# Attention values and softmax sums taken in 32-column quarters of TensorE, with a wide reciprocal on VectorE

## The reference

```
h = layernorm(x) * (1 + ca) + sa
x = x + ga * attention(h)          # 16 heads of 16; 4 sink keys and the last 128 keys
h = layernorm(x) * (1 + cb) + sb
x = x + gb * (shared_ffn(h) + sum over the top 2 of 16 experts of weight * expert(h))
```

## Time and profile before

| what | us |
|---|---|
| median of 3 runs | 353.09 (351.51 to 356.67) |
| the profiled execution | 351.6 |
| its span | 349.8 |
| PE busy | 280.7 (80%) |
| DVE busy | 232.1 (66%) |
| POOL busy | 204.4 (58%) |
| ACT busy | 162.4 (46%) |

### The profile page before, as it was taken

One profiled execution on the slowest core, in us unless ns is written; L12 is line 12 of the kernel. 1 busy time (PEld: TensorE's weight loads), 2 busy tenths in 40 slices (PEclk: granted clock), 3 DMA queues, 4 the chain that ended last, 5 costly groups with the idle time before them and its releaser, 6 DMA issues.

```text
span 349.8 us, 6292 instructions
## 1 busy us (share of the span) xinstructions
PE 280.7 (80%) x1665; PEld 218.9 (63%) x1666; DVE 232.1 (66%) x899; ACT 162.4 (46%) x518; POOL 204.4 (58%) x254
## 2 busy tenths in 40 slices
PE   4897889888989898988873998999899898986000
PEld 4174467655857486756642897889889787875000
DVE  0468477997789876997894654644354576862990
ACT  3042552278135743457213355555455565753540
POOL 3604107738775577648657364556556468783981
PEclk9998996999789987999988799999999999998755
DMA  7939101123615529802275663555557678757894
GB/s 265 325 95 361 33 2 60 62 77 121 195 46 165 166 92 340 191 15 85 85 211 186 204 173 107 151 153 162 150 154 222 192 243 262 233 171 274 287 358 163
DMA packets 41438, 59.80 MB, mean 171 GB/s; under 512 B 5092, under 2 KB 29880, under 8 KB 41404
## 3 DMA queue, kind: packets, MB, share of 16 engines
q1 hardware_dynamic: 34312, 39.91, 38.8%
q0 software_dynamic: 6528, 17.90, 14.3%
q10 hardware_dynamic: 564, 1.59, 1.3%
HBM read 33.57 MB, written 25.80 MB: 170 GB/s over the span
## 4 chain that ended last, share of the span: by engine, by line
PE 49%; DVE 23%; issue 8%; DMA 7%; ACT 5%; another core or an unknown queue 2%; SPq 2%; POOL 1%; DVEq 1%; POOLq 0%; ACTq 0%
PE bank L1225 15%; PE bank L1235 7%; PE bank L890 7%; PE bank L1050 5%; PE bank L1083 5%; PE bank L1027 2%; PE bank L1103 2%; DVE h_sb L1367 2%; DVE st L1341 2%; PE bank L933 2%; DMA ht<-in_L_attn_x_dram 2%; ACT pt_win L674 2%; DVE xs L1389 1%; ACT p_win L717 1%
## 5 line engine op out<-in xcount | busy, mean ns | idle before, releaser
L646 POOL DMA_INDIRECT ys<-pt_win,row_i x72 | 71.5, 992 | 52.2 <-issue 25.9
L1225 PE MATMUL bank<-ht,w_now 128*128 128x128 f32 x576 | 79.2, 282 | 5.6 <-issue 4.5
L593 POOL DMA_INDIRECT slots<-h_sb,slot_i x64 | 63.2, 988 | 31.3 <-DVE slot_i L1438 16.0
L1225 PEld LDWEIGHTS bank<-ht,w_now 128*128 128x128 f32 x576 | 73.0, 198 | 6.8 <-issue 5.1
L1736 DVE TENSOR_TENSOR act_t<-bank,sg 128x128 f32<-128x128 f32 x72 | 20.9, 291 | 49.0 <-ACT sg L841 33.6
L674 ACT ACTIVATE ht<-bank 128x256 f32<-128x256 f32 x104 | 39.9, 383 | 22.4 <-PE bank L890 12.9
L1235 PE MATMUL bank<-w_dn,act_t 128*128 x144 | 45.2, 396 | 4.3 <-DVE act_t L1736 3.8
L674 ACT ACTIVATE pt_win<-bank 128x256 f32<-128x256 f32 (+1 forms) x88 | 37.3, 423 | 21.0 <-PE bank L1235 8.3
L1083 PE MATMUL bank<-w_route,ht 128*128 128x272 f32 x128 | 41.5, 452 | 4.3 <-ACT ht L674 1.8
L890 PE MATMUL bank<-ident,p_win 128*128 128x128 f32 x198 | 36.0, 277 | 5.5 <-issue 2.8
L890 PEld LDWEIGHTS bank<-ident,p_win 128*128 128x128 f32 x198 | 26.6, 143 | 19.2 <-issue 7.7
(11 more groups left out here) (260 smaller groups left out, 490.1 us busy)
## 6 DMA issues: line engine op xcount, KB each, us to landing
p_win<-slots SPq DMA_DIRECT2D x67, 129.0 KB
slots<-pads SPq DMA_DIRECT2D x28, 129.0 KB
xs<-in_L_attn_x_dram SPq DMA_DIRECT2D x3, 1024.0 KB
wmod_sb<-ys SPq DMA_DIRECT2D x12, 256.0 KB
w_gu<-ys SPq DMA_DIRECT2D x10, 256.0 KB, 2.8
mod_bc<-mod_rows_out SPq DMA_DIRECT2D x4, 512.0 KB, 5.4
w_dn<-in_L_ffn_w_down_dram SPq DMA_DIRECT2D x1, 2048.0 KB
h_sb<-ys SPq DMA_DIRECT2D x8, 256.0 KB
```

The source lines that it names most:

```text
L593: pool.indirect_dma_start(out=slots, out_offset=bass.IndirectOffsetOnAxis(ap=slot_i[:, k, j:j + 1], axis=0), in_=h_sb[:, j, :], in_offset= ...
L646: pool.indirect_dma_start(out=ys, out_offset=bass.IndirectOffsetOnAxis(ap=row_i[:, col:col + 1], axis=0), in_=y_sb[:, k, :], in_offset=Non ...
L1225: last = mm(bank[2 + k % 2][:, half * P:(half + 1) * P], w_now[:, k % 2, c, half * M:(half + 1) * M], ht[:, k, c, :], start=(c == 0), stop ...
```

## The change

`at_values` is turned round. The values of two heads stand in 32 stationary columns, with zeros beside them (`v_pad`), and the transposed probabilities are the moving operand. Each product writes 32 of the 128 output partitions, so that four products fill the four quarters of a bank. The output comes out transposed, as `at_project` needs it: `at_out_t` and ACT's copy are gone. The sums come from a second set of products with ones in place of values (`at_sums`, `ones_pad`, `sink_ones`), 256 moving columns each. They give every sum 16 times over, in the layout of the output, and DVE takes the reciprocal of all 128x256 elements. The setup gets the matching constants, and the products of the few sink rows (`small_values`) get their sums from matmuls of their own.

The order moves too. On PE: `at_sums`, `at_values`, `gate_up(b, 5)`, `rank`, `at_project`, `tr`, `act_tr`, `down`. On DVE: `at_norm(b + 1)` goes in front of `activation(b, 4)`, `at_normalise` in front of `ranked` and `placed`, and the statistics of the next batch's first tiles behind `activation(b, 5)`. On POOL: `last_norm` goes ahead of `scale(b, 6)`, and `rsqrt(b, 2)` ahead of the next batch's `scale` calls. On ACT: `h_copy(b, 5)` and `act_copy(b, 5)` go ahead of `centre(b + 1, 0)` and `centre(b + 1, 1)`.

```diff
@@ constants and tiles
-    DA = DH + 1
+    PAIR_STEP = 2 * DH
+    V_HALF = CH * PAIR_STEP + DH
-        sink_v = sb("sink_v", [H * SINKS, B * H * DA])
+        sink_v = sb("sink_v", [H * SINKS, B * D])
+        sink_ones = sb("sink_ones", [H * SINKS, D])
-        v_aug = sb("v_aug", [P, H, DA])
+        v_pad = sb("v_pad", [P, 2 * V_HALF])
+        ones_pad = sb("ones_pad", [P, 3 * DH])
-        rden = sb("rden", [P, H])
+        rden = sb("rden", [P, D])
@@ pool
+                if b + 1 < B:
+                    last_norm(b + 1)
                 if b == 0:
                     rsqrt(b, 3)
                 scale(b, 6)
...
                 if b + 1 < B:
-                    last_norm(b + 1)
                     rsqrt(b + 1, 0)
+                rsqrt(b, 2)
+                if b + 1 < B:
...
                     scale(b + 1, 0)
                     scale(b + 1, 1)
-                rsqrt(b, 2)
@@ act
                 tanh(b, 5)
-                act.wait_ge(S["at_ot"], b + 1)
-                copy(o_t[:].rearrange("p c n -> p (c n)"), bank[6][:, 0:D]).then_inc(S["at_ots"], 1)
+                h_copy(b, 5)
+                act_copy(b, 5)
                 if b + 1 < B:
                     centre(b + 1, 0)
                     centre(b + 1, 1)
-                act_copy(b, 5)
-                h_copy(b, 5)
@@ pe
+            def at_sums(b):
+                wait_apart(pe, S["at_pts"], b * (HG + 1) + HG + 1)
+                for c in range(C):
+                    mm(bank[6][:, c * P:(c + 1) * P], sink_ones[:, c * P:(c + 1) * P], pt_sink[:], start=(c == 0),
+                       stop=False, skip_group_check=True)
+                for u in range(2):
+                    for i in range(4):
+                        last = mm(bank[6][32 * i:32 * i + 32, 0:D], ones_pad[:, (1 - u) * DH:(3 - u) * DH],
+                                  pt_win[:, 2 * i + u::CH, :], start=False, stop=(u == 1), skip_group_check=True)
+                last.then_inc(S["at_den"], 1)
+
+            def at_values(b):
+                for c in range(C):
+                    mm(bank[7][:, c * P:(c + 1) * P], sink_v[:, ds(b * D + c * P, P)], pt_sink[:], start=(c == 0),
+                       stop=False, skip_group_check=True)
+                for c in range(C):
+                    for u in range(2):
+                        for i in range(4):
+                            v_at = u * (V_HALF - DH) + (c * 4 + i) * PAIR_STEP
+                            last = mm(bank[7][32 * i:32 * i + 32, c * P:(c + 1) * P], v_pad[:, v_at:v_at + PAIR_STEP],
+                                      pt_win[:, c * CH + 2 * i + u, :], start=False, stop=(u == 1),
+                                      skip_group_check=True)
+                last.then_inc(S["at_o"], 1)
@@ order on pe
-                at_values(b, range(0, H // 2))
+                at_sums(b)
+                at_values(b)
+                gate_up(b, 5, b == 0)
                 rank(b * GPB, 0, GROUP, b * TPB + 2)
-                at_values(b, range(H // 2, H))
-                gate_up(b, 5, b == 0)
-                at_out_t(b)
-                act_tr(b, 5, b == 0)
                 at_project(b)
                 tr(b, 5)
+                act_tr(b, 5, b == 0)
@@ dve
             def at_normalise(b, at):
+                dve.wait_ge(S["at_den"], b + 1)
+                at.done(v.reciprocal(rden[:], bank[6][:, 0:D]))
                 dve.wait_ge(S["at_o"], b + 1)
-                ob = bank[7][:, 0:H * DA].rearrange("q (h s) -> q h s", h=H)
-                at.done(v.reciprocal(rden[:], ob[:, :, DH]))
-                v.tensor_tensor(o_n[:], ob[:, :, 0:DH], rden[:].unsqueeze(2).to_broadcast([P, H, DH]), ALU.mult)\
+                v.tensor_tensor(o_t[:].rearrange("p c n -> p (c n)"), bank[7][:, 0:D], rden[:], ALU.mult)\
                     .then_inc(S["at_on"], 1)
@@ order on dve
                 add_y(b, 3)
+                if b + 1 < B:
+                    at_norm(b + 1, at)
                 activation(b, 4)
...
+                at_normalise(b, at)
                 ranked(b * GPB)
                 placed(b * GPB)
-                if b + 1 < B:
-                    at_norm(b + 1, at)
-                    norm_stats(b + 1, 0, ln)
-                at_normalise(b, at)
                 if b == B - 1:
                     early_table(0)
                 activation(b, 5)
+                if b + 1 < B:
+                    norm_stats(b + 1, 0, ln)
```

More of the change, by code:

```diff
@@ L135, in norm_of @@
             return 0 if j < 2 else 2 if j == TPB - 1 else 3 if b == 0 and j == TPB - 2 else 1
-        norms = ["a0", "00", "10", "30"]
-        for b in range(B):
+        norms = ["a0", "00", "10", "a1", "30", "01", "20", "11"]
+        for b in range(1, B):
             norms += [f"a{b + 1}", f"0{b + 1}", f"2{b}", f"1{b + 1}"] if b + 1 < B else [f"2{b}"]
@@ L750, in own_values @@
                 act.wait_ge(S["at_v"], b + 1)
-                copy(v_aug[:, :, 0:DH], bank[6][:, 0:D].rearrange("p (h s) -> p h s", s=DH))\
+                copy(v_own, bank[6][:, 0:D].rearrange("p (m u s) -> p u m s", u=2, s=DH))\
                     .then_inc(S["at_vs"], 1)
@@ L989, in small_values @@
                 for b in range(B):
-                    last = mm(bank[3][0:NB, 0:H * DA], sm_pt[:, b, :], sink_v[:, b * H * DA:(b + 1) * H * DA],
-                              start=(b == 0), stop=(b == B - 1))
+                    mm(bank[3][0:NB, 0:D], sm_pt[:, b, :], sink_v[:, b * D:(b + 1) * D], start=(b == 0), stop=False,
+                       skip_group_check=True)
+                for b in range(B):
+                    last = mm(bank[3][0:NB, D:D + H], sm_pt[:, b, :], head_block[:], start=False, stop=(b == B - 1),
+                              skip_group_check=True)
                 last.then_inc(S["sm_ps"], 1)
@@ L1042, in at_probs_t @@
                 last.then_inc(S["at_pt"], 1)
[L1044 to L1051, removed]
-                if heads[-1] == H - 1:
-                    last.then_inc(S["at_o"], 1)
@@ L1055, in at_out_t @@
-            def at_out_t(b):
-                pe.wait_ge(S["at_on"], b + 1)
-                for k in range(C):
-                    last = transpose(bank[6][:, k * P:(k + 1) * P],
-                                     o_n[:].rearrange("q h s -> q (h s)")[:, k * P:(k + 1) * P])
-                last.then_inc(S["at_ot"], 1)
-            def at_project(b):
-                pe.wait_ge(S["at_ots"], b + 1)
+            def at_sums(b):
[8 more added lines that the diff above has]
+                last.then_inc(S["at_den"], 1)
@@ L1064, in at_project @@
+            def at_project(b):
+                pe.wait_ge(S["at_on"], b + 1)
                 for k in range(C):
@@ L1521, in small_normalise @@
                 dve.wait_ge(S["sm_ps"], 3)
-                so = bank[3][0:NB, 0:H * DA].rearrange("q (h s) -> q h s", h=H)
-                ch.done(v.reciprocal(sm_r[:], so[:, :, DH]))
-                v.tensor_tensor(sm_o[:], so[:, :, 0:DH], sm_r[:].unsqueeze(2).to_broadcast([NB, H, DH]), ALU.mult)\
+                so = bank[3][0:NB, 0:D].rearrange("q (h s) -> q h s", h=H)
+                ch.done(v.reciprocal(sm_r[:], bank[3][0:NB, D:D + H]))
+                v.tensor_tensor(sm_o[:], so, sm_r[:].unsqueeze(2).to_broadcast([NB, H, DH]), ALU.mult)\
                     .then_inc(S["sm_or"], 1)
@@ L1668, in _ @@
                 add_y(b, 3)
+                if first:
+                    dve.wait_ge(ld_x[1], 16)
+                if b + 1 < B:
+                    at_norm(b + 1, at)
                 activation(b, 4)
@@ L1795, in _ @@
                 gated(d)
-N_CONST = 32
+N_CONST = 34
 RT_CH = 9
```

17 lines of the change are left out of this document (11 added, 6 removed).

## The result

The changed kernel took 355.19 us (median of 20 runs, 352.48 to 358.69), the kernel before beside it 354.57 (20 runs, 350.37 to 358.97). The ratio is 1.0055, with a 95% interval from 1.0028 to 1.0081: half a per cent slower, far inside the 2% called no change. The predicted 357 was 1.8 us too high. But 357 was worked out as 3.7 us on top of a kernel before of 353.1; in this comparison the kernel before took 354.6, and the ratio makes the change worth some 2 us. The direction was right, but the case given the best chance, pairs, isn't what happened.

What follows compares the result with a forecast made beforehand. Bound: PE from the sinks' product through the projection, then DVE. Batches -0.1, -0.2, 0.0, +2.5, setup +0.1 and clock +1.4 give +3.7 on 351.6 profiled: 355.3, plus 1.5 for the median: 356.8, said as 357; range 348 to 366.

Steps and rivals of the forecast that it cites:

- pairs: Quarter products on PE run two at a time: sums 1.94 us, values 1.84, stage 5.4; chance 0.42.
- What bounds the kernel: Batch 1's chain runs on PE from 88.28 to 98.65, then on DVE; a faster PE alone gives at most 2.76 us.
- four at a time: Rival: all four quarters overlap on PE, stage 3.3 us, DVE bounds; 349 profiled, 350.7; chance 0.22.
- Changes of shape: Switching product shapes on PE costs 0.15 us each, five per stage: 0.75 us.
- Reciprocal: 256 columns on DVE take 1.76 us, 1.5 more per batch, needing only the sums; hidden if quarters overlap two at a time.
- The old fall of the clock: Half clock during the heads' narrow products goes if wide streams keep it up; a fall cost 3.0 us at the projection's end.
- A new fall in PE's idle: PE idles some 3 us before `down(b, 6)` in batches 0 to 2, clock falls: 0.7 for two of them, +1.4 us.
- `rank` behind `gate_up(b, 5)`: `rank` is seen 6.65 us after the stage's start; `ranked`, `placed` and DVE's queue wait, total 13.65 us.
- POOL: "nothing": Scatters wait for `placed`, some 4 us later, yet fit with two rsqrts and two scales before the next batch: no cost.
- Batch 3: No half clock to regain, and `early_table(0)` waits for the count from `rank`: `activation(3, 5)` starts 2.5 us later.

Runs made afterwards that it cites:

- The test in one quarter: Changed kernel with all quarter products written to the first 32 rows of their bank; 366.1 us, one run.
- the narrow one: Changed kernel with a reciprocal of 16 columns in place of 256; 344.82 us, ratio 1.0034 to the kernel before.
- filler alone: Changed kernel plus six bf16 products of 512 columns in PE's idle before `down` of tile 6, every batch; 341.60 us, ratio 0.9980 to the kernel before.
- rank first: Changed kernel with `rank` between `at_sums` and `at_values`, `ranked` and `placed` before `at_normalise`; 339.13 us, ratio 0.9786 to the kernel before; repeat 337.97, 0.9803.

## Why the prediction was right, and where it was wrong

- **What bounds the kernel**: right. The edited stage was on the path; with it faster, DVE's idle went.
- **Pairs** (chance 0.42): wrong. Sums and values take 1.0 us each and not 1.94 and 1.84. The step that failed is the ordering argument, that the second record of an f32 product must wait for the first before the next quarter can go. The test in one quarter (3.64 us) and the rows of the changed kernel (1.07) say four at a time. The figure that the prediction cited beside it (the Trainium skill, "TensorE: Matmul & The Clock Gate", Part 3) points the right way: it gives 2.38 times for three column tiles. The runs here give 3.4 for four (3.64 / 1.07); none has three.
- **Changes of shape**: right as a sum. The stage is 3.3 us, what the rival had for it with 0.15 each.
- **Reciprocal**: right in price (1.76 us) and place. It waits 0.46 us for the sums. Its load isn't what ate the gain, as the narrow one shows.
- **The old fall of the clock goes**: right in all batches.
- **A new fall in PE's idle**: right in kind; it shows in `gate_up` of tile 7 in batches 0, 1 and 3 (62.2, 100.2, 179.4 us), and one tile later in batch 2 (143.4). But its price of +1.4 us isn't there: filler alone moved no spacing, and all that `gate_up` gained by it was idle (1.82 us) until DVE's `h_sb`, late behind POOL.
- **`rank` behind `gate_up(b, 5)`**: this order costs, as forecast, but by another way: rank first gives 5.6 us back. On DVE there is no wait for `rank` in batch 1, since the reciprocal and the product stand in front; the cost comes through POOL.
- **POOL: "nothing"**: wrong, and the most instructive step. The prediction said that four scatters, two roots and two scales "fit before the next batch needs them", and looked at the scales' consumer alone. The first consumer is `h_tile(b, 7)`, which waits for the root. On POOL's queue, one by one from `slot_i` at 94.16: the issues end at 99.7, the roots at 100.96, and DVE wants them at 99.9. The trace of before had the means to see it: slots 4 us later by its own estimate, four scatters 1.27 us apart (92.49 to 97.30), and `centred` right behind `activation(b, 6)`.
- **Batch 3**: +0.8 us to the end of `activation(3, 6)` and 0.7 to the start of `activation(3, 5)` (7.04 us after the sinks for 6.30), where pairs had +2.5 and four at a time +0.7.
- **The number**: the rival of four at a time had 350.7 us: -1.3, -2.0, -1.3 in batches 0 to 2. The first stretch gave more, -2.4, -2.7, -1.8. What it lacked is POOL's +2.0 in each of three batches and up to 0.9 behind it, which has no cause here. Its sum with these is 350.7 - 2.3 + 6.0 + 2.1 = 356.5, or 355.1 without the clock's 1.4. That 357 is close is luck in large part: products too dear by 2.1 us a batch and a queue too cheap by 2 us cancel, and the kernel before came out 1.5 us slower than the 353.1 that the sum started from. Against that kernel the forecast was +3.7 us, and the measured ratio gives some +2.

## What to carry to other kernels

When a step is moved later, count what is queued behind it on every engine that it feeds, one instruction at a time, and ask which consumer of that queue comes first, not which seems the natural one. Three waits stood here one behind the other (POOL's root, the landing of a scatter behind bulk loads, DVE beside POOL's scales); taking the first two away, from behind, gave 3 us of spacings in the end (113.9 to 110.8), and putting the small row product and the slots ahead of the wide work gave 5.6 (to 108.3). And the releaser that a profile names is only the last that it sees: where a wait has two conditions, look up the landing time in the queue's rows too.

## What the hardware showed

- Products in four column quarters run side by side even in f32: 32 records of 128 columns in 1.08 us, 3.68 when all use one quarter.
- DVE instructions of 0.2 to 0.4 us grew to 1.8 and 2.16 us when POOL's scales ran: `counted_b` (two inputs in SBUF) and `at_xn_sb` (one input, f32) end as POOL's pair of scales ends. That is by the Trainium skill, "SBUF — State Buffer", section "SBUF: two separate sides": the port pair of DVE and GpSimd is locked for a whole instruction, for DVE instructions with two SBUF inputs or in a two-port mode, and the loser blocks. The times agree with a block, but no trace shows a port or which mode `at_xn_sb` ran in. Here the loser seems to have waited for three POOL instructions in a row (a root and two scales), and a `centred` that met the first scale only until that one ended. It wasn't tested by itself.
- A scatter of 128 rows lands 2.5 us after its issue (median) in a quiet stretch and 8.5 behind 3.5 MB of bulk transfers on another queue; with those moved away it is 2.6.
- Six filler products of 512 bf16 columns (1.46 us) in a gap of 1.84 us kept the granted clock at 2.4 GHz; the `gate_up` behind it took 1.08 us instead of 2.02. Without filler the clock fell behind that gap in batches 0 and 1, and in batch 2 in one trace of two. With rank first the gap was 1.46 us in batch 1, and the clock stayed up without filler in batches 0 to 2.
